# Moving the second layer's attention projections: three chunks into the first FFN, the last between the second attention's first scores

## The reference, cut to what matters

```python
x = x + layernorm(attention0(layernorm(x)))   # MLA-like attention, 16 heads of 16
x = x + layernorm(ffn0(layernorm(x)))         # silu(x Wg * sg) * (x Wu * su) -> Wd * sd, inner width 1024
x = x + layernorm(attention1(layernorm(x)))   # qkv = x Wqkv + b, 16 heads of 16, causal softmax
x = x + layernorm(ffn1(layernorm(x)))
```

## Time and profile before

| | us |
|---|---|
| Median of three runs (lowest, highest) | 1278.7 (1278.65, 1279.92) |
| The profiled execution, its device time | 1275.28 |
| Its span, first to last instruction | 1273.5 |

### The profile page before, as it was taken

The page is one execution under the profiler, slowest core; times in us unless marked ns, Lnnn a source line. Parts: engine busy times, 40 slices in busy tenths (PEclk is TensorE's granted clock), DMA queues, the critical chain, the costliest instruction groups (busy, mean ns, idle before and its releaser), DMA issues.

```text
span 1273.5 us, 35512 instructions
## 1 busy us (share of the span) xinstructions
PE 1164.4 (91%) x14872; PEld 586.6 (46%) x14872; DVE 1049.9 (82%) x2746; ACT 720.6 (57%) x919; POOL 334.7 (26%) x561
## 2 busy tenths in 40 slices
PE   5769999999999998799978789999999999987996
PEld 4432344544444543566645224455444445454664
DVE  7759999999999862878863899999999988558776
ACT  2441377767677886234342407777767778843332
POOL 2321211122111133433442212111231112424433
PEclk9976699999999999899999659999999999997998
DMA  5354000211100000000026320021120000000000
GB/s 173 121 160 109 25 15 15 64 28 37 43 3 2 3 4 3 18 16 1 1 77 190 85 87 15 15 56 28 30 58 4 3 3 3 4 1 2 17 18 33
DMA packets 31600, 49.95 MB, mean 39 GB/s; under 512 B 7245, under 2 KB 24143, under 8 KB 31431
## 3 DMA queue, kind: packets, MB, share of 16 engines
q1 hardware_dynamic: 25376, 41.95, 11.9%
q0 software_dynamic: 5488, 5.34, 1.4%
q10 hardware_dynamic: 576, 0.39, 0.1%
HBM read 32.56 MB, written 14.68 MB: 37 GB/s over the span
## 4 chain that ended last, share of the span: by engine, by line
PE 68%; DVE 19%; DMA 4%; ACT 3%; POOL 3%; issue 2%; SPq 1%; ACTq 0%; POOLq 0%; DVEq 0%
PE ps L887 65%; DVE m_tile L780 6%; DVE ps L782 3%; DMA k_parts<-parts 2%; DVE region_p L640 1%; DVE stats L627 1%; ACT region_p L569 1%; DMA q_parts<-parts 1%; PE ps L1034 1%; POOL q_stack L455 1%; DVE region_p L838 1%; PE ps L882 1%; DVE rem L681 1%; POOL parts L423 1%; DVE region_p L754 1%
## 5 line engine op out<-in xcount | busy, mean ns | idle before, releaser
L569 ACT ACTIVATE region_p<-ps 128x1024 f32<-128x1024 f32 (+3 forms) x640 | 541.4, 894 | 246.9 <-PE ps L887 243.4
L780 DVE TENSOR_REDUCE m_tile<-ps 128x1 f32<-128x512 f32 x768 | 501.3, 685 | 28.0 <-PE ps L887 22.5
L887 PE MATMUL ps<-k_stack,q_stack 96*32 96x512 bf16 (+3 forms) x5120 | 435.2, 375 | 21.4 <-DVE v_all L688 7.6
L887 PE MATMUL ps<-q_stack,k_stack 99*32 99x512 bf16 (+3 forms) x5120 | 350.5, 352 | 3.6 <-ACT region_p L569 2.2
L887 PE MATMUL ps<-region_p,v_all 128*17 128x512 f32 (+3 forms) x2560 | 292.8, 531 | 5.0 <-POOL region_p L460 4.8
L782 DVE CUSTOM_DVE_ANT_0 ps<-ps,causal 128x128 f32<-128x128 f32 (+3 forms) x512 | 248.7, 497 | 27.8 <-PE ps L887 26.3
L887 PEld LDWEIGHTS ps<-k_stack,q_stack 96*32 96x32 bf16 x5120 | 144.0, 96 | 256.5 <-DVE m_tile L780 104.0
L887 PEld LDWEIGHTS ps<-q_stack,k_stack 99*32 99x32 bf16 x5120 | 140.3, 98 | 153.3 <-issue 56.7
L460 POOL TENSOR_SCALAR_AFFINE_SELECT region_p<-region_p 128x512 f32<-128x512 f32 x128 | 81.1, 635 | 275.3 <-ACT region_p L569 269.7
L887 PE MATMUL ps<-region_a,w_ffn 128*128 128x512 f16 x512 | 125.8, 392 | 6.1 <-DVE region_a L672 5.2
L603 ACT ACTIVATE k_stack<-ps,cols 128x512 f32<-128x512 f32 x64 | 44.0, 688 | 129.9 <-PE ps L887 125.2
(11 more groups left out here) (93 smaller groups left out, 895.6 us busy)
## 6 DMA issues: line engine op xcount, KB each, us to landing
k_parts<-parts SPq DMA_DIRECT2D x16, 384.0 KB, 7.9
q_parts<-parts SPq DMA_DIRECT2D x16, 384.0 KB, 8.7
q_stack<-q_parts SPq DMA_DIRECT2D x32, 192.0 KB
k_stack<-k_parts SPq DMA_DIRECT2D x32, 192.0 KB
q_stack<-q_parts SPq DMA_DIRECT2D x32, 128.0 KB
k_stack<-k_parts SPq DMA_DIRECT2D x32, 128.0 KB
X<-in_x SPq DMA_DIRECT2D x4, 512.0 KB, 6.6
q_stack<-q_parts SPq DMA_DIRECT2D x32, 64.0 KB
```

The source lines that it names most:

```text
L569: nc.scalar.activation(probs[:, o.j % SLOTS, 2 * o.hp:2 * o.hp + 2, o.off:CH], psT[:, o.k % 2, :, o.off:CH], ACT.Exp, scale=SCALE).then_in ...
L780: nc.vector.tensor_reduce(maximum, scores, AX.X, ALU.max).then_inc(s.ring_free, 1)
L887: return pe.matmul(o, a, b, start=first, stop=last)
```

## The change

The diff has some 520 lines; these are its parts.

1. **Order of units.** Layer 1's 16 units are now chunk by chunk, four each. Twelve of them (`EARLY = 12`) and six of the eight `v` products are made during FFN 0. `early_jobs(u)` says at which unit of the following chunk: branch at i = 2, statistics, normalisation, transposes ("x"), two pairs of units and two `v` products at the next six positions, one later for chunks 0 and 1.
2. **Banks.** Side work in both FFNs (the transposes of `x16`, "x", units, `v`) alternates between banks 6 and 7; a job waits until the one two before it has been drained (`side_release`). The transposed chunk goes to `x_chunk`, two buffers in `region_p`.
3. **FFN positions.** The square root of the branch goes from i = 3 to i = 2, its normalisation from i = 4 to 2, POOL's four additions from i = 4 and 5 to i = 2, in both layers.
4. **The last chunk.** Its transposes stand at turn 3 of the second attention, its four units at turns 8, 10, 12, 14, its two `v` products at turn 16; their DVE and POOL work at turns 10 to 20.
5. **Group 1's stacks**, in both layers, wait for step 2's first `T`.

```diff
+    STEP2_T = min(o.k for o in ORDER if o.kind == "T" and o.n == 2)
+        x_chunk = region_p[:, NT * C:NT * C + 2 * KC * CH].rearrange("p (b k t) -> p b k t", b=2, k=KC)
-            [("qk", m, c) for c in range(NCH) for m in (0, 2)] + [("qk", m, c) for c in range(NCH) for m in (1, 3)],
+            [("qk", m, c) for c in range(NCH) for m in (0, 2, 1, 3)],
+        EARLY = 12
+        def early_jobs(u):
+            jobs = []
+            for d in range(NCH - 1):
+                i = u - NI * (d + 1)
+                late = 1 if d < NCH - 2 else 0
+                jobs += [(job, d) for job, at in (("branch", 2), ("stats", 3 + late), ("norm", 4 + late), ("x", 5 + late),
+                                                  ("pair0", 6 + late), ("pair1", 7 + late), ("rest", 8 + late)) if at == i]
+            return jobs
+        X_AT, UNITS_AT, VALUES_AT, FIRST_T = 3, {8: 12, 10: 13, 12: 14, 14: 15}, 16, min(
+            n for n, o in enumerate(ORDER) if o.kind == "T")
+        REM_AT, VALUES_SB_AT, LOW_AT = {10: 12, 12: 13, 14: 14, 16: 15}, 20, {15: (12, 13), 16: (14, 15)}
...
@@ sync @@
-                sp.wait_ge(s.t_filled, L * T_N + 1)
+                sp.wait_ge(s.t_filled, L * T_N + STEP2_T + 1)
...
@@ gpsimd, FFN loop @@
-                    if i in (4, 5) and c > 0:
-                        for t in range(2):
-                            add_residual(2 + 2 * L, TPC * (c - 1) + 2 * (i - 4) + t)
+                    if i == 2 and c > 0:
+                        for t in range(TPC):
+                            add_residual(2 + 2 * L, TPC * (c - 1) + t)
+                    for job, d in early_jobs(u) if L == 0 else []:
+                        if job == "pair0":
+                            split_lo(1, 4 * d)
+                        if job == "pair1":
+                            split_lo(1, 4 * d + 1)
+                            split_lo(1, 4 * d + 2)
+                        if job == "rest":
+                            split_lo(1, 4 * d + 3)
...
@@ tensor, before the second attention @@
+                    side(0, "v", 4)
+                    side(0, "v", 5)
+                    pe.wait_ge(f.evac, NT)
+                    pe.wait_ge(p.v_sb, 6)
...
@@ tensor, FFN loop @@
-                    if i == XHAT_AT[c] + 2:
-                        transpose_batch(k1, c + 1)
+                    for kind, n in side_jobs(L, u):
+                        side(L, kind, n)
```

More of the change, by code:

```diff
@@ L266, in build_program, with v_after, chunk_ready, chunk_units @@
         VU = NT // 2
[L267 to L275, removed]
+        EARLY = 12
+        def v_after(u):
+            n = VU // (NU - EARLY)
+            return range((u - EARLY) * n, (u - EARLY + 1) * n) if u >= EARLY else range(0)
+        def chunk_ready(L, u):
+            if L == 0:
+                return (u - 1) // 3 - 1 if u % 3 == 1 and 4 <= u <= 13 else None
+            return u // 4 if u % 4 == 3 else None
+        def chunk_units(L, c):
+            return 3 * (c + 1) if L == 0 else 4 * c + 2
         def unit_dram(L, u):
@@ new lines, in side_jobs @@
+        def side_jobs(L, u):
+            c, i = divmod(u, NI)
+            jobs = [("x16", 2 * c + 2), ("x16", 2 * c + 3)] if u < NCH * NI and i == XHAT_AT[c] + 2 else []
+            for job, d in early_jobs(u) if L == 0 else []:
+                if job == "x":
+                    jobs += [("x", 2 * d), ("x", 2 * d + 1)]
+                if job in ("pair0", "pair1"):
+                    first = 4 * d + 2 * (job == "pair1")
+                    jobs += [("unit", first), ("unit", first + 1)]
+                if job == "rest":
+                    jobs += [("v", 2 * d), ("v", 2 * d + 1)]
+            return jobs
@@ new lines, in build_program, with side_bank, side_release, unit_bank @@
+        UF = NCH * NI
+        SIDE = [[("x16", 0), ("x16", 1)] + [j for u in range(UF + 1) for j in side_jobs(L, u)] for L in range(2)]
+        def side_bank(L, kind, n):
+            return 6 + SIDE[L].index((kind, n)) % 2
+        def side_release(L, kind, n):
+            return {"x16": (turn[1 + 2 * L].moved_v, n + 1), "x": (turn[2].moved_a, n + 1),
+                    "unit": (proj[1].rem, n + 1), "v": (proj[1].v_sb, n + 1)}[kind]
+        def unit_bank(L, u):
+            if L == 1:
+                return side_bank(0, "unit", u) if u < EARLY else (u + 2) % 4
+            return u % 4
@@ L354, in _ @@
                     sp.dma_start(unit_dram(L, u), parts[:, u % PB, :, :]).then_inc(parts_stored[L][u % PB], 16)
[L355 to L358, removed]
+                    c = chunk_ready(L, u)
+                    if c is not None:
+                        parts_complete(chunk_units(L, c))
+                        load_stacks(0, c)
                 parts_complete(NU)
@@ L430, in _ @@
             for L in range(2):
-                for u in range(NU):
-                    split_lo(L, u)
-                for o in ORDER:
+                if L == 0:
+                    for u in range(NU):
+                        split_lo(0, u)
+                for at, o in enumerate(ORDER):
+                    for u in LOW_AT.get(at, ()) if L == 1 else ():
+                        split_lo(1, u)
                     if o.kind == "S" and o.last:
@@ L762, in _ @@
                     chunk = {"down": chunk_down, "z": chunk_z, "c": chunk_ckv}
[L763 to L768, removed]
-                base = L * RING_N
-                for o in ORDER:
+                    for u in range(NU):
+                        for what, c in DVE_BEFORE.get(u, []):
+                            chunk[what](c)
+                        unit_rem(0, u)
+                        for v in v_after(u):
+                            v_value(0, v)
+                base = L * RING_N
+                for at, o in enumerate(ORDER):
+                    if L == 1 and at in REM_AT:
+                        unit_rem(1, REM_AT[at])
+                    if L == 1 and at == VALUES_SB_AT:
+                        v_value(1, 6)
+                        v_value(1, 7)
                     if o.kind == "S":
@@ L1065, in _ @@
                 k1 = 1 + 2 * L
[L1066 removed]
+                side(L, "x16", 0)
+                side(L, "x16", 1)
                 f = ffn[L]
```

168 lines of the change are left out of this document (114 added, 54 removed).

## The result

The changed kernel takes **1313.6 us** (median of 4 runs, 1312.43 to 1314.48); the kernel before, on the same chip, 1278.68 (1277.83 to 1279.92). The ratio is 1.0272, 95% interval 1.0254 to 1.029: 34.9 us slower. The forecast was 1301 within 1285 to 1313, so the sign was right, and the time lies 0.6 us above the range. The profiled execution took 1314.48 us, its span is 1312.7 and its mean granted clock 0.928 (0.942 before).

What follows compares the result with a forecast made beforehand. It took PE to set the first FFN's pace and a DMA chain to bound the stage behind it. Tail -20, last chunk +7 and late stacks +35 make +22 on 1278.7: 1300.7, given as 1301, range 1285 to 1313.

Steps and rivals of the forecast that it cites:

- Part A: Projections moved into the first FFN, which grows by 29 us; with the tail and last chunk, a gain of 13.
- rival 3: Stalls of 8 us in the FFN, last chunk at half clock, 19; total 1312; chance 0.13 together with rival 4.
- The tail: From the FFN's last `down` to the second attention's first drain: first drain at 688.5, 20.0 us gained.
- The last chunk among the scores: Four units and two `v` products between turns 8 and 16 of the second attention: a cost of 7 us.
- I take 7: The cost in us taken for the last chunk among the second attention's scores, ends 4.6 and 19.
- which may give 2.5 back: After the last chunk's units, a busy PE starts the next scores and first `T`s at full clock: 2.5 us back.
- Part B: Late stacks of group 1: PE stands ahead of step 4's first score, 17.5 us a layer, 35 for both.
- the 24 us bound: Upper end of Part B's loss per layer, if group 1's load takes 38.6 us.
- Fast loads: Group 1's stacks load in 21 us, stall 4.8 + 1 a layer ahead of step 4; 1278; chance 0.08.
- stacks that are no limit: Group 1's stacks land before step 4's first score, so Part B costs nothing; 1266; chance 0.09.
- loss of 5: The bad end for Part A with its tail and last chunk: 5 us lost instead of 13 gained.
- rival 4: DVE or ACT runs full inside the FFN and PE waits, at rival 3's price or more; chance 0.13 together with rival 3.

Runs made afterwards that it cites:

- e5: e1 with group 0's last chunk of stack loads held until the first `T` in the second layer; 1271.21 us, ratio 0.9953.
- e6: e1 with the last chunk's units at turns 10, 16, 22, 25 and its `v` products at 27; 1273.42 us, ratio 0.9962.
- e1: The changed kernel with group 1's stacks loaded after the first `T` of all again, in both layers; 1270.95 us, ratio 0.9955.
- e2: The kernel before with only group 1's stacks made to wait for step 2's first `T`; 1317.7 us, ratio 1.0319.
- e8: The kernel before with only the broadcast query loads split into pieces of 16 partitions; 1255.78 us, ratio 0.9841.
- e10: e8 repeated, on the chip of a kernel combining all edits; 1256.85 us, ratio 0.9839.
- e7: e1 with the broadcast query loads split into pieces of 16 partitions; 1259.35 us, ratio 0.986.
- e3: The changed kernel with group 1's stacks triggered at step 1's first `T` instead of step 2's; 1280.91 us, ratio 1.0018.

## Why the prediction was right in sign and low in size

- **Part A, the FFN: held.** 29 us forecast, 27.8 measured; a pair of units between FFN units took 3.60 us, 1.80 each. The stalls for which I took 1.5 us (rival 3: 8) are about that: the one new wait of PE is that of the transposes, 2.1 us in three.
- **The tail: held.** From the FFN's start to the first drain 21.35 us gained, 20.0 forecast. The last `down` ended at 699.2; less the 26.2 us by which everything is late there, 673.0 (forecast 674.2), and the first drain 687.1 (688.5). DVE started `down_out` 4.3 us behind that end (4.4) and needed 9.9 us from there (9.9). PE's wait for the load of ones was not foreseen and hid behind DVE's work. The wait of the high parts for a DMA is gone.
- **The last chunk among the scores: this step failed.** "I take 7": it measured 15.9. Its first half was sized well: turns 8 to 20 took PE 16.9 us (716.73 to 733.65) where I had 15.7, the first unit was at the lower clock as assumed, and step 0's drains (turns 0 to 15) grew from 7.6 to 16.05 us, by 8.4. What failed is the sentence behind it, "which may give 2.5 back": instead, the way from step 0's maxima to step 1's grew from 18.2 to 25.6 us, by 7.4. DVE's rows show where: it waited 2.05 us for PE behind the `v` products and 3.18 for the first `T`, 5.9 in all with some short waits where it was 0.7 before, and it had 2.15 us of moved work of its own. I had followed PE and DVE and not the small chain behind the maxima, which grew from 7.4 to 14.5 us. The `v` products and the scores of turns 16 to 20 stand ahead of MT (733.80), DVE's drain of `v` 6 and 7 ahead of the copy (735.93), and of the four DMAs the last lands in 5.59 us: group 0's stacks of chunk 3, issued at 733.45 because their stores come only now, share the engines with it. Nor did the clock help. It was at its full level from 723 to 735, the last three of these us with PE busy for only 1.70, between waits for DVE's drains. From 735 it was at the lower one, six us ahead of PE's wait for the row, and the first `T`s ran at 0.50 as they had in the kernel before:

```profile
735.00:738.00 3.00, 1.72 (x16) 0.44 (x16) 2.93 (x10) 2.53 (x2) 1.57 (x3) 0.51 0.48 144
```

  e5 gives the DMA's share, 3.1 us of the 7.1 by which the `T` came later; that the other 4.1, by which the copy came later, are order (MT, drains) is argued from the rows, not tried alone, and e6 shows only that spreading the units doesn't lessen the sum.
- **Part B: held, each layer somewhat low.** 17.5 us a layer forecast, 19.0 measured. The time left for the load was 16.2 and is 16.3 (804.02 to the end of PE's work at 820.3); the load took 33.6 us (804.02 to 837.57) for 32; and behind the gap, 17.25 us, another 1.8 were lost where I had 1.5. The forecast's own terms, 15.8 and 1.5, make 17.3. Twice the 1.5 us between 17.5 and 19.0 is 3 us. e1 and e2 show the cause both ways; the 24 us bound for a load of 38.6 was not reached.
- **The sum.** -21.35 + 15.9 + 38 = +32.6, where the prediction has +22: of the 10.6 us, 8.9 are the last chunk, 3.0 Part B, -1.35 the tail. The medians have +34.9; the other 2.3 are not placed.
- **The rivals.** Fast loads and stacks that are no limit are out: both need a load of 21 us or less, and it took 33.6. Rival 3 named the right place, the last chunk among the scores (its 19 against 15.9 measured), and had 8 us of stalls in the FFN, which did not come. Its total, 1312, came nearest to the time, but only by a slip: its -20 has no last chunk in it yet, so Part A comes to -20 + 6.5 + 19 = +5.5, the "loss of 5" of the prediction's own ends, and its sum to 40.5: 1319. The projections were hidden, so rival 4 is out.
- **The range.** Its upper end, 1313, was taken from that total. Summed rightly it would have been 1319 and would have held the 1313.6; the miss by 0.6 us hangs on the slip as much as on the last chunk. The other end of Part A, a gain of 22, does not come out of its terms either: 20 + 1.5 - 4.6 is 16.9.
- **What I did not see:** that the wide broadcast loads were also what bound the stage of projections before. I read that the stores share SP's queue with stack loads and priced the queue's order, not the loads' rate; e8 and e10 show that 21 us of the kernel before lay in it, about half of them in each layer, where the moved projections brought 6.8.

## What to carry to other kernels

When a load is triggered later, write down two numbers from the trace: from trigger to first use, and from first issue to that use when nothing is spare. Here 16 against 33 us gave the loss within 10%, and an engine that works in order stands for all of the difference. Before work is moved to hide a chain of DMAs, look at the shape of the DMAs in it: here a few lines that split the broadcast loads were worth 21 us, a rebuilt schedule 7 without them and -4 to -5 with them. And work that is put between the first scores delays the rows of maxima, which come to PE by way of DVE, POOL, PE, DVE and a DMA: price the time to the first use of the maxima, not the engine that is full.

## What the runs showed of the hardware that was not expected

- The same bytes with three or two of the slowest dimension or with 16: from first issue to the score that needs the last, 33.6 against 21.7 us (33.2 against 21.5 in the first layer), though SP issues 36 DMAs instead of 24. Stores of 384 KB issued among them landed in 9.5 us and in 3.3.
- The last of four DMAs of maxima, 3 KB each, landed in 5.59 us while the stacks of one chunk were under way (5.74 in e1), and in 3.25 in e7, where those are narrow.
- Of e3's ten runs two lie near 1274 us and seven near 1281, with one between. What chooses is open.
